# Message stage of a graph kernel: ranges of 32 nodes in four column tiles of TensorE

## The reference

```python
sh1 = sqrt(3) * edge_vectors / (r + 1e-09)                 # one direction per edge, 3 numbers
h = silu(edge_lengths_embedding @ fc_w1 / sqrt(NB))
w = (h @ fc_w2 / sqrt(NH)).reshape(-1, 5, 64)              # five weights of 64 per edge
s = node_features[:, :64][sender]
v = node_features[:, 64:].reshape(-1, 64, 3)[sender]
dot = einsum('eui,ei->eu', v, sh1)
crs = cross(v, sh1[:, None, :])
m0 = (w[:, 0] * s + w[:, 3] * dot / sqrt(3)) / sqrt(2)
m1 = (w[:, 1] * s * sh1 + w[:, 2] * v + w[:, 4] * crs / sqrt(2)) / sqrt(3)
agg0, agg1 = segment_sum of m0 and m1 over the receiver, / 16
out = concat(agg0 @ lin_w0, agg1 @ lin_w1) + node_features
```

## Time and profile before

| | us |
|---|---|
| median of 3 runs | 2762.05 |
| lowest, highest | 2761.53, 2766.91 |
| profiled execution, first to last instruction | 2736.8 |
| TensorE busy in it | 2107.6 (77%) |
| VectorE busy | 2183.1 (80%) |
| ScalarE busy | 1524.3 (56%) |
| GpSimd busy | 1618.3 (59%) |

### The profile page before, as it was taken

One profiled execution on the slowest core, in us unless ns is written; L12 is line 12 of the kernel. 1 busy time (PEld: TensorE's weight loads), 2 busy tenths in 40 slices (PEclk: granted clock), 3 DMA queues, 4 the chain that ended last, 5 costly groups with the idle time before them and its releaser, 6 DMA issues. The chain is left out here.

```text
span 2736.8 us, 41806 instructions
## 1 busy us (share of the span) xinstructions
PE 2107.6 (77%) x9647; PEld 1611.0 (59%) x9647; DVE 2183.1 (80%) x3415; ACT 1524.3 (56%) x4291; POOL 1618.3 (59%) x1808
## 2 busy tenths in 40 slices
PE   3999999999999999679815666666566666656666
PEld 2787878777777777533314455455455545545555
DVE  6888888888888888645546878878888788878793
ACT  5787888788877887433223444444444444444443
POOL 5666666666666666342246666666666666666642
PEclk8999999999999999889957788878878878887787
DMA  6232222222222222769856666666666666666651
GB/s 203 72 84 81 83 83 83 83 82 84 83 83 81 84 82 84 167 165 253 234 181 168 168 173 175 173 165 173 177 169 175 169 172 176 167 175 170 173 141 45
DMA packets 157414, 379.08 MB, mean 139 GB/s; under 512 B 47810, under 2 KB 63298, under 8 KB 157186
## 3 DMA queue, kind: packets, MB, share of 16 engines
q0 software_dynamic: 100544, 309.00, 40.6%
q1 hardware_dynamic: 44946, 68.53, 8.7%
q10 hardware_dynamic: 11904, 1.34, 0.4%
HBM read 353.36 MB, written 37.07 MB: 143 GB/s over the span
## 5 line engine op out<-in xcount | busy, mean ns | idle before, releaser
L1358 POOL DMA_INDIRECT kv_e<-kv_rows,edge x752 | 716.9, 953 | 408.4 <-issue 223.4
L487 POOL DMA_INDIRECT feat<-in_x_rows,idx x664 | 677.1, 1020 | 236.2 <-issue 234.8
L523 ACT ACTIVATE vsh<-feat,rec_a 128x256 f32<-128x256 f32 x1980 | 806.8, 495 | 8.9 <-DMA feat<-in_x_rows,idx 4.8
L1541 PE MATMUL ps_sum<-kv_e,ident 128*128 128x264 f32 x1504 | 473.8, 477 | 376.9 <-issue 264.2
L1541 PEld LDWEIGHTS ps_sum<-kv_e,ident 128*128 128x128 f32 x1504 | 352.5, 240 | 481.8 <-issue 283.6
L571 PE MATMUL ps_a<-msg,hot 128*128 128x257 f32 x1312 | 409.4, 393 | 4.0 <-issue 4.0
L573 PE MATMUL ps_a<-msg,hot 128*128 128x256 f32 x1312 | 390.6, 379 | 0.1
L575 PE MATMUL ps_a<-msg,hot 128*128 128x192 f32 x1312 | 320.2, 325 | 0.0
L573 PEld LDWEIGHTS ps_a<-msg,hot 128*128 128x128 f32 x1312 | 248.6, 190 | 38.2 <-issue 1.9
L575 PEld LDWEIGHTS ps_a<-msg,hot 128*128 128x128 f32 x1312 | 248.8, 190 | 34.9
L571 PEld LDWEIGHTS ps_a<-msg,hot 128*128 128x128 f32 x1312 | 222.2, 189 | 66.3 <-issue 66.3
(11 more groups left out here) (419 smaller groups left out, 3182.2 us busy)
## 6 DMA issues: line engine op xcount, KB each, us to landing
ef<-in_ef_t SPq DMA_DIRECT2D x84, 256.0 KB
kv_e<-kv_rows,edge POOLq DMA_INDIRECT x752
rows_e<-rows SPq DMA_DIRECT2D x41, 272.0 KB
feat<-in_x_rows,idx POOLq DMA_INDIRECT x664
rows_e<-in_ef_t SPq DMA_DIRECT2D x1, 7446.0 KB, 26.6
kv_rows<-kv SPq DMA_DIRECT2D x20, 260.0 KB, 2.5
rows_e<-in_ef_t SPq DMA_DIRECT2D x1, 3706.0 KB
x<-x_rows SPq DMA_DIRECT2D x23, 128.0 KB
```

Of the source, the lines that this page charges most:

```text
L487: pool.indirect_dma_start(out=feat[:, u, c, 0, :, :].rearrange("p a b -> p (a b)"), out_offset=None, in_=g.x_rows, in_offset=bass.Indirect ...
L523: ins = act.activation(vsh[:, u % TURN, c, j, :, :], feat[:, u % TURN, c, 0, :, :], ACT.Copy, scale=rec_a[:, u % 2, c, 1 + j:2 + j])
L1358: pool.indirect_dma_start(out=kv[:, u, s, :], out_offset=None, in_=g.kv_rows, in_offset=bass.IndirectOffsetOnAxis(ap=edge[:, u, s, DH + 1: ...
L1541: mm = pe.matmul(out, g.ident[:], kv[:, u, s, D:], start=(s == 0), stop=False, skip_group_check=True)
```

## The change

- A range is now 32 nodes, starting every 16. A step handles one super-chunk in one range. Codes are super-chunk number x 256 + range number; the tables stage is adapted, and makes three placing matrices `g.place` and a matrix `g.wide`.
- The one-hot has 32 columns per edge. It is made four times: as it is, and multiplied by each of the three numbers of the edge's direction. ScalarE's 12 scalings and VectorE's dot and cross products are gone; the directions are in the one-hots, and products of them with the message parts add up to dot and cross products in PSUM.
- `scatter` does 28 products a step: chunk c goes to the 32-column tile c of the array and to the partitions 32c to 32c+31 of the one bank `ps_a`. Terms with a minus sign are gathered in separate columns.
- ScalarE copies `ps_a` to SBUF (`part`, the minus columns negated) and lays out `fold`; `gathered` sums the four quarters and puts them in their place by two products into `ps_f`. VectorE adds `ps_f` to `g.sums`, three steps later than the products were made.
- The sender numbers are copied by ScalarE instead of GpSimd, four steps ahead.
- A window's sums lie in three slabs: one to three products more in `stage_order` and six instead of four in `turn_sums`.

```diff
-HALVES = 2 * WINDOWS
-SPAN = 64
-IDLE = HALVES
+REACH = 32
+UNIT = REACH // 2
+QUARTERS = P // REACH
+UNITS = NODES_PAD // UNIT
+SLABS = UNITS // QUARTERS + 2
+SPAN = 256
+IDLE = UNITS
...
-TABLE = -(-(SUPERS * WINDOWS + 2 * TURN) // 512) * 512
+LAG = 3
+TABLE = -(-(SUPERS * (-(-NODES // REACH)) + 16) // 512) * 512
...
-    nodes = g.iota_node[:, bass.ds(w * (P // 2), P)].rearrange("p (a n) -> p a n", a=1).broadcast_to([P, CHUNKS, P])
-    receivers = g.rec[:, bass.ds(sc * CHUNKS, CHUNKS), 0:1].broadcast_to([P, CHUNKS, P])
+    nodes = g.iota_node[:, bass.ds(w * UNIT, REACH)].rearrange("p (a n) -> p a n", a=1).broadcast_to([P, CHUNKS, REACH])
+    receivers = g.rec[:, bass.ds(sc * CHUNKS, CHUNKS), 0:1].broadcast_to([P, CHUNKS, REACH])
...
-        hot = sb("hot", [P, 2, CHUNKS, P])
-        msg = sb("msg", [P, 2, CHUNKS, 3 * D + 1])
+        hot = sb("hot", [P, 2, 4, CHUNKS, REACH])
+        msg = sb("msg", [P, 2, CHUNKS, WIDTH])
+        part = sb("part", [P, 2, LESS + D + 1])
+        fold = sb("fold", [P, 2, P])
...
-        ps_a = ctx.enter_context(nc.psum_tensor("ps_a", [P, 2, 512], F32))
+        ps_a = ctx.enter_context(nc.psum_tensor("ps_a", [P, 512], F32))
+        ps_f = ctx.enter_context(nc.psum_tensor("ps_fold", [P, 512], F32))
...
-                    if c == 1:
-                        senders(i + 1, (u + 1) % TURN)
...
+                    gather(t * TURN + u + TURN, u)
...
-                        ins = act.activation(vsh[:, u % TURN, c, j, :, :], feat[:, u % TURN, c, 0, :, :], ACT.Copy,
-                                             scale=rec_a[:, u % 2, c, 1 + j:2 + j])
...
+                for u in range(TURN):
+                    i = t * TURN + u
+                    _sc, w = step_of(nc, act, g.code, i)
+                    act.wait_ge(m_prod, i + 1 + TURN)
+                    senders(i + TURN, u)
+                    silu(i + 2, u)
+
+                    act.wait_ge(m_fold, i + 2)
+                    at = nc.s_assert_within(act.snap((QUARTERS - 1 - w % QUARTERS) * REACH), 0, (QUARTERS - 1) * REACH,
+                                            skip_runtime_bounds_check_because="one of four places")
+                    act.activation(fold[:, u % 2, :], g.wide[:, bass.ds(at, P)], ACT.Copy)
+                    act.wait_ge(m_used, i + 3)
+                    act.activation(part[:, u % 2, LESS:], ps_a[:, LESS:LESS + D + 1], ACT.Copy)
+                    act.activation(part[:, u % 2, 0:LESS], ps_a[:, 0:LESS], ACT.Copy, scale=-1.0).then_inc(m_out, 1)
 
...
+            def scatter(u):
+
+                for c in range(CHUNKS):
+                    out = ps_a[c * REACH:(c + 1) * REACH, :]
+                    pe.matmul(out[:, LESS:LESS + D + 1], hot[:, u % 2, 0, c, :], msg[:, u % 2, c, 0:D + 1], start=True,
+                              stop=False, skip_group_check=True)
+                for j in range(3):
+                    plus, minus = TURNS + (j + 2) % 3 * MUL, TURNS + (j + 1) % 3 * MUL
+                    for c in range(CHUNKS):
+                        out = ps_a[c * REACH:(c + 1) * REACH, :]
+                        dots = DOTS + j * MUL
+                        pe.matmul(blocks(out, LESS + 1, (1 + (j + 1) % 3) * MUL), hot[:, u % 2, 1 + j, c, :],
+                                  blocks(msg[:, u % 2, c, :], dots, plus - dots), start=False, stop=False,
+                                  skip_group_check=True)
+                    for c in range(CHUNKS):
+                        out = ps_a[c * REACH:(c + 1) * REACH, :]
+                        less, more = (j + 2) % 3 * MUL, LESS + 1 + (1 + j) * MUL
+                        mm = pe.matmul(blocks(out, less, more - less), hot[:, u % 2, 1 + j, c, :],
+                                       blocks(msg[:, u % 2, c, :], minus, SIDE - minus), start=False, stop=(j == 2),
+                                       skip_group_check=True)
+                mm.then_inc(m_used, 1)
+
+            def gathered(u):
+
+                out = ps_f[:, 0:D + 1]
+                pe.matmul(out, fold[:, u % 2, :], part[:, u % 2, LESS:], start=True, stop=False, skip_group_check=True)
+                pe.matmul(out[:, 1 + MUL:], fold[:, u % 2, :], part[:, u % 2, 0:LESS], start=False, stop=True,
+                          skip_group_check=True).then_inc(m_fold, 1)
...
+                    pe.wait_ge(m_out, i + 1)
+                    scatter(u)
+                    pe.wait_ge(m_acc, i + 2)
+                    gathered(u + 1)
...
+            def add_sums(i, w):
+
+                slab = g.sums[:, bass.ds(w // QUARTERS + 1, 1), :].rearrange("p a d -> p (a d)")
+                dve.wait_ge(m_fold, i + LAG + 1)
+                dve.tensor_tensor(slab, slab, ps_f[:, 0:D + 1], ALU.add).then_inc(m_acc, 1)
...
-                    dve.tensor_tensor(dot, v[:, :, 0, 1, :], v[:, :, 1, 2, :], ALU.add).then_inc(m_dot, 1)
-                    dve.tensor_tensor(f[:, :, 1, 1, :], v[:, :, 2, 2, :], v[:, :, 1, 3, :], ALU.subtract)
-                    dve.tensor_tensor(f[:, :, 1, 2:4, :], cut(at(0, 3), D - 2 * MUL), cut(at(2, 1), MUL - 2 * D),
-                                      ALU.subtract).then_inc(m_cross, 1)
-                    dve.wait_ge(m_dot, i * 2 + 1)
-                    dve.tensor_tensor(dot, dot, v[:, :, 2, 3, :], ALU.add).then_inc(m_dot, 1)
...
+                    one_hots(dve, g, hot[:, u % 2, 0], sc, w).then_inc(m_hot, 1)
+                    dve.wait_ge(m_hot, i + 1)
+                    same = hot[:, u % 2, 0:1].broadcast_to([P, 3, CHUNKS, REACH])
+                    axes = g.rec[:, bass.ds(sc * CHUNKS, CHUNKS), 1:].rearrange("p c (j a) -> p j c a", a=1)
+                    dve.tensor_tensor(hot[:, u % 2, 1:], same, axes.broadcast_to([P, 3, CHUNKS, REACH]), ALU.mult)
+                    add_sums(i - LAG, w_before)
+
+                    m = msg[:, u % 2]
...
+                    dve.wait_ge(m_snd[u], t * (16 * CHUNKS) + 16 * CHUNKS)
+                    dve.tensor_tensor(own, wt[:, :, 0:2, :], f[:, :, 0:1, :].broadcast_to([P, CHUNKS, 2, MUL]), ALU.mult)
+                    for a, at in ((2, AXES), (3, DOTS), (4, TURNS)):
+                        out = m[:, :, at:at + 3 * MUL].rearrange("p c (b d) -> p c b d", b=3)
+                        ins = dve.tensor_tensor(out, wt[:, :, a:a + 1, :].broadcast_to([P, CHUNKS, 3, MUL]), f[:, :, 1:4, :],
+                                                ALU.mult)
+                    ins.then_inc(m_prod, 1)
...
+                for k, slab in enumerate((1, 2, 0)):
+                    ins = act.activation(agg[:, k, :], g.sums[:, bass.ds(w * 2 + slab, 1), 1:].rearrange("p a d -> p (a d)"),
+                                         ACT.Copy)
+                ins.then_inc(p_agg, 1)
...
-                    pe.matmul(ps_a[:, cols], agg[:, cols], g.ident[:], start=True, stop=False, skip_group_check=True)
-                    mm = pe.matmul(ps_a[:, cols], beside[:, cols], g.swap[:], start=False, stop=True, skip_group_check=True)
+                    for n in range(3):
+                        mm = pe.matmul(ps_a[:, cols], agg[:, n, cols], g.place[:, n, :], start=(n == 0), stop=(n == 2),
+                                       skip_group_check=True)
```

More of the change, by code:

```diff
@@ L262, in _ @@
             r2, r3 = 1.0 / np.sqrt(2.0), 1.0 / np.sqrt(3.0)
-            for path, scale in enumerate((r2, r3 * r2, r3, r3 * r2, r3)):
+            for path, scale in enumerate((r2, r3, r3, r3 * r2, r3 * r2)):
                 cols = g.w2[:, :, path * MUL:(path + 1) * MUL]
@@ L567, in _ @@
                         hidden_pair(u + 2, t * (16 * TURN // 2) + 16 * (u // 2 + 2))
-                    out = ps_a[:, u % 2, :]
-                    for c in range(CHUNKS):
-                        rows = msg[:, u % 2, c]
-                        pe.matmul(out[:, 0:D + 1], hot[:, u % 2, c, :], rows[:, 2 * D:3 * D + 1], start=(c == 0),
-                                  stop=False, skip_group_check=True)
-                        pe.matmul(out[:, 0:D], hot[:, u % 2, c, :], rows[:, D:2 * D], start=False, stop=False,
-                                  skip_group_check=True)
-                        mm = pe.matmul(out[:, MUL:D], hot[:, u % 2, c, :], rows[:, MUL:D], start=False,
-                                       stop=(c == CHUNKS - 1), skip_group_check=True)
-                    mm.then_inc(m_used, 1)
+                    pe.wait_ge(m_out, i + 1)
+                    scatter(u)
+                    pe.wait_ge(m_acc, i + 2)
+                    gathered(u + 1)
+            pe.wait_ge(m_out, turns * TURN + 1)
+            pe.wait_ge(m_acc, turns * TURN + 2)
+            gathered(1)
         @block.vector
@@ L725, in _ @@
         def _(pe):
-            pe.wait_ge(r_prior, 2)
-            pe.matmul(ps_p[:, 32:32 + WINDOWS], g.swap[:], beside[:], start=True, stop=True).then_inc(r_first, 1)
+            for k, slab in enumerate((1, 2, 0)):
+                mm = pe.matmul(ps_p[:, 32:32 + WINDOWS], g.place[:, k, :], g.sums[:, slab:slab + 2 * WINDOWS:2, 0],
```

(2 more changed lines are left out.)

188 lines of the change are left out of this document (81 added, 107 removed).

## The result

The changed kernel took 3037.22 us (3031.14 to 3042.72) where the kernel before took 2761.79 (2759.22 to 2766.91) beside it: ratio 1.1001, 95% interval 1.0973 to 1.1028. It is 275 us slower, where 206 us less was forecast and the range ended at 2710. The slower result came again in two later groups (e5, e15); the faster one rests on the two runs of e18, and e1, a variant, agrees with it. I call the two kinds of place, by the time of the kernel before, the 2762 place and the 2522 place. Only the first had been seen when the prediction was made.

A forecast was written before the change was run, and what follows sets the result against it. TensorE was taken to bound the message stage at 6.535 us a step, falling to 5.2 by gathers: 159 steps save 212 us; 2736.8 - 212 + 6 = 2531, plus 25.25 gives 2556 us, range 2500 to 2710.

The forecast's parts named there:

- TensorE's 4.5 us: Message step on TensorE: weights 1.28, hidden pair 0.31, scatter 1.9, fold 0.85, waits 0.2; 2 us less than before.
- the loop's 4.8: Message step: product ends, weights, then VectorE's products of 3.28 us close a loop of 4.8 us through one bank set.
- GpSimd's 5.2: Message step: four indirect gathers, 5.02 us at the least and 5.27 by the mean; expected to bound next.
- ScalarE's 2.6: Message step: ScalarE loses 4.9 us of scaling, gains copies and code reading, and needs 2.6 us with L509.
- The slower rival: Scatter's 56 passes don't overlap, 6.89 or 5.9 us; 3245 us (3080) in total; decides above 3.9 us; chance 0.16.
- the rival with two tiles: Scatter: only two column tiles overlap, 3.44 us, TensorE's step 6.1 us, 2699 us in total; chance 0.19.
- The overlap of four column tiles: Scatter: four column tiles run side by side, so 56 passes take 1.9 us, with ends 1.72 and 6.89.
- The 62 ns for each matmul with hardware decoding off: Scatter: a quoted sequencer cost by which 56 passes take about 3.5 us, the same outcome as two tiles overlapping.
- Setting L1035's rows aside: Scatter: L1035's two column tiles gained nothing, but read with a stride of 16 elements; L553 was taken as nearer.
- Weights and hidden pair: TensorE's message step: 1.28 us for the weights and 0.31 a step for the hidden pair.
- +6: Outside the message stage: 5 us more for the projection stage's extra products and 1 for the tables stage.
- The 25.25 us from the span to the median: Whole kernel: median 2762.05 us stands 25.25 above the profiled span 2736.8; kept and added to 2531 for the total.

The follow-up runs named there:

- e5: The changed kernel, unaltered, run again beside the kernel before: 3035.92 us against 2762.45, ratio 1.098.
- e15: The changed kernel, unaltered, run once more in a later group: 2980.72 us, beside 2765.39 for the kernel before.
- e18: The changed kernel, unaltered, in the last group: 2280.06 us, beside 2522.05 for the kernel before, ratio 0.904.
- e1: Changed kernel with two steps instead of four in TensorE's message-stage loop: 2283.43 us against 2524.57 for the kernel before, ratio 0.9047.
- e4: Kernel before with eight steps instead of four in TensorE's message-stage loop: 2547.92 us, beside 2524.57 for the kernel before.
- e12: Kernel before with 36 products of one column added to each message step: 3930.93 us, beside 2765.39 for the kernel before.
- e2: Changed kernel without the message stage's gathers and the wait for them: 2240.25 us, beside 2524.57 for the kernel before.
- e7: Changed kernel without the message stage's gathers and the wait for them, in a later group: 2474.17 us, beside 2762.45 for the kernel before.
- e11: Changed kernel with two of the four gathers of a message step: 2615.15 us, beside 2742.1 for the kernel before.

## Why the prediction was wrong, and where it was right

**The step that failed** is the choice of 5.2 us for the message step out of four bounds (TensorE's 4.5 us, the loop's 4.8, GpSimd's 5.2, ScalarE's 2.6). It left out a fifth: TensorE starts its instructions more slowly while gathers run, the more so the more instructions a step has. At the 2762 place that gives 8.25 us for 140 records and four gathers, 7.08 for 92 and four, 5.73 for 140 and two, 4.81 for 140 and none. That this is their supply is the likeliest reading and no more. The prediction put the term at nothing. The long passes of the kernel before are no proof of that: they show only that 68 records in 6.5 us are supplied. A row that may speak of it was on the page, in a stage that I didn't cost: groups by line of the kernel before, and of e4 (the same kernel but for its loop) at the 2522 place; behind the stroke the idle time and what ended most of it:

```profile
L1541 PE MATMUL ps_sum<-kv_e,ident 128*128 128x264 f32 x1504 | 473.8, 477 | 376.9 <-issue 264.2
```

```profile
L1542 PE MATMUL ps_sum<-kv_e,ident 128*128 128x264 f32 x1504 | 458.1, 470 | 278.3 <-DVE kv_e L1779 278.1
```

In the attention stage of the kernel before TensorE idles 264 us for "issue" at the 2762 place and waits for VectorE alone at the other. From the last message step to the end that kernel takes 1616 us at the one (1636 in e12) and 1408 at the other: 208 to 228 of the 240 us between the places are there, while its message step is the same at both (6.53 and 6.51 us).

**The slower rival** had the right spot, the scatter, and the right deciding point, and the wrong mechanism. It said slower once the 56 passes take more than 3.9 us; they took 4.5. The doubt that 56 passes with 56 loads are "handed over so quickly" stands in the rival with two tiles; both rivals asked it of the array and of a steady rate of passes. Neither is the limit: the passes that are there run at full rate. What was missing is a hold that depends on another engine's gathers. Its price, 3080 to 3245 us, was above the measured 3037.

**The overlap of four column tiles**, on which the prediction was said to stand or fall, held: one line's records at the 2762 place (min, median and max ns, the same three at the other):

```profile
L583 PE MATMUL ps_a<-msg,hot x8: 380/392/404, 709.4 to 709.7; 128*32 128x257 f32 x8
```

Eight passes of 257 columns in 0.46 us are 0.057 each, where one alone needs 257 x 0.84 ns = 0.22. The scatter is 1.88 us up to the fold, 1.9 forecast; from its first pass to the start of its last 1.68. Two tiles at a time would have been 3.44. The 62 ns for each matmul with hardware decoding off, which the prediction quotes from the Trainium skill, "TensorE: Matmul & The Clock Gate", section "Wait — 56ns, not 53.3ns?", aren't seen in the burst: eight passes of L590 in 0.22 us are 0.028 each; over the whole step, 70 passes in 4.97 us or 0.071 each, they can't be excluded. Setting L1035's rows aside came out right; that its stride is why they gained nothing is tested by no run.

**The other terms**, read at the 2522 place. Weights and hidden pair 1.49 (1.28 + 0.31 = 1.59 forecast). Gathers, from e18's timeline of GpSimd:

```profile
500.25 0.95 POOL L506 DMA_INDIRECT feat<-in_x_rows,idx  x1 [0.30 <-issue]
501.50 0.94 POOL L506 DMA_INDIRECT feat<-in_x_rows,idx  x1 [0.30 <-issue]
502.75 0.95 POOL L506 DMA_INDIRECT feat<-in_x_rows,idx  x1 [0.30 <-issue]
```

1.25 us each, without a gap between steps as foreseen; four are 5.0, the lower end of 5.02 to 5.27. I had taken 5.2 by the message stage's 1017 ns, but the index copy between them went away too, and the attention stage's 0.95 was the row to use. So the step is 4.97, and bounded by the gathers with the loop of weights and products (4.81 in e2) close under them. Projection and all stages behind the messages: 1408 us before (e4) and after (e18), so +6 was 0. The 25.25 us from the span to the median are 1.7 in e18: they were the distance between two executions and no fixed part of a time. Kept in the sum, they only make the saving be taken from the median, which is sound. The saving is 2522 - 2280 = 242 us for 206 forecast.

**The clock** was ranked as a rival at full supply; at the 2522 place it stays at 1.00 with TensorE 89% busy. At the other it is 0.87, and e7 and e11 have 1.00 there, without gaps and with shorter ones. So it isn't the cause.

**Range and chances.** The working was right for a place that I hadn't seen and wrong for the one whose profile I had. That it held at the 2522 place is no merit of the forecast, which knew of one place only. A chance of 0.17 for slower was too little: the instruction count of the bound engine doubled from 68 to 140 a step while its time was to fall by a third, and no row showed that density beside gathers.

## What to carry to other kernels

Count the instructions a us that a change asks of an engine, and look for a stretch of the same profile where it gets that many beside the same GpSimd gathers; idle time ended by "issue" anywhere on that engine is the sign to look for. Many short products in place of few long ones are a bet on this supply: it won 9.6% in one place and lost 10% in another. Compare only variants that ran side by side, with the kernel in question among them.

## What was not expected of the hardware

- Places that run the kernel before in 2522 and in 2762 us differ in none of the durations compared (a gather of L506 951 and 949 ns, L583's passes 380 to 404 at both) but in what stands between them: two groups of runs found the one kind, four the other (2742 to 2765).
- At the 2762 kind gathers on GpSimd hold up TensorE, which shares no data with them at that moment: with two gathers a step 1.7 gaps a step of 0.6 us each, with four passes 0.7 or 1.4 us apart. Half the bytes change nothing (8.04 us); no gathers, no gaps.
- In the scatter shown above 31 passes and their 31 loads went through before the first gap. The Trainium skill, "Advanced Engine Details and Errata", section "Engine Queue Depths", gives TensorE a queue of 64 and calls it complicated with tiling; it would be such a store, filled while TensorE waits for VectorE. The trace doesn't bear out a fixed number: of 90 scatters 28 have no gap of over 0.5 us, and the others have 17 to 55 passes before the first. That the long passes of the kernel before live on this store is argued only.
- A product of one column of 64 rows costs 0.058 us a pass with its load at 2.4 GHz, as much as a pass of 257 columns on one of four column tiles (0.057).
